# Loading the next batch's context, x and first two weights during the last MLP, and waiting for the stores one batch later

## What is computed

```
x = L0(x, ctx)   # x1 = LN(x) Wq, ctx Wk, ctx Wv, 16 heads; + x; then LN and an MLP of 2048, + residual
x = L1(x, ctx)   # 32 query heads on 8 key heads, additive mask, + x, then LN with gamma and beta
x = L2(x, ctx)   # LN(ctx) as keys and values; x + tanh(gate) * out
x = L3(ctx, x)   # keys and values over [ctx, x], queries from x; RMSNorm, MLP of 2048, + x
```

## Time and profile before

| | |
|---|---|
| median of 3 runs | 4301.14 us (4297.38 to 4302.05) |
| the profiled execution's own time | 4311.11 us |
| its span, first to last instruction | 4309.5 us |
| busy: PE, DVE, ACT, POOL | 87%, 35%, 27%, 7% of the span |
| mean granted TensorE clock | 0.943 of full |
| transfers of the 16 DMA engines | 271.10 MB, 63 GB/s mean |

### The profile page before, as it was taken

How to read it: one execution, slowest core, us unless ns; L and a number is a source line. 1 busy time by engine, 2 the same in 40 slices (tenths; PEclk the granted TensorE clock), 3 DMA queues, 4 the chain that set the end, 5 groups by cost and what they waited for, 6 DMA issues and landing times. The chain is left out here.

```text
span 4309.5 us, 39566 instructions
## 1 busy us (share of the span) xinstructions
PE 3736.4 (87%) x14128; PEld 1798.2 (42%) x14128; DVE 1525.2 (35%) x2792; ACT 1183.0 (27%) x1404; POOL 293.4 (7%) x228
## 2 busy tenths in 40 slices
PE   5998988889799898878979989887897989988799
PEld 2444533334344553333434455333343445533334
DVE  2415443530340544343034054434303305443430
ACT  1312323241131232324113133222412313322340
POOL 3000011000100001100010000110001000011000
PEclk9999999999899999989989999998998999999899
DMA  6322153311622215331162221533116221153401
GB/s 125 66 88 40 21 103 48 59 32 50 126 68 82 36 23 101 47 64 28 51 126 65 84 34 26 99 55 59 25 54 128 66 82 31 25 99 55 68 16 59
DMA packets 151761, 271.10 MB, mean 63 GB/s; under 512 B 15520, under 2 KB 22372, under 8 KB 151544
## 3 DMA queue, kind: packets, MB, share of 16 engines
q1 hardware_dynamic: 151556, 268.35, 30.8%
HBM read 152.95 MB, written 4.19 MB: 36 GB/s over the span
## 5 line engine op out<-in xcount | busy, mean ns | idle before, releaser
L908 ACT ACTIVATE pt<-score_banks 128x1024 f32<-128x1024 f32 x768 | 761.0, 1022 | 950.3 <-PE score_banks L769 482.4
L639 PE MATMUL bank<-xT,w 128*128 128x512 f32 x1664 | 755.4, 601 | 38.3 <-ACT xT L881 23.4
L1038 DVE TENSOR_REDUCE mcol<-bank 128x1 f32<-128x512 f32 x528 | 359.3, 689 | 469.7 <-PE bank L737 466.2
L639 PEld LDWEIGHTS bank<-xT,w 128*128 128x128 f32 x1664 | 315.9, 192 | 396.5 <-issue 370.4
L765 PE MATMUL score_banks<-qs,ks 99*128 99x512 f32 (+1 forms) x1280 | 450.7, 429 | 23.6 <-DMA qs<-nm_lo 12.6
L737 PE MATMUL bank<-ks,qs 97*128 97x512 f32 (+1 forms) x784 | 344.8, 453 | 137.7 <-DMA ks<-k_full 49.5
L1021 DVE TENSOR_REDUCE mcol<-score_banks 128x2 f32<-128x1024 f32 x248 | 301.7, 1223 | 426.2 <-PE score_banks L728 411.6
L838 PE MATMUL score_banks<-w,wide 128*128 128x512 f32 x1024 | 443.4, 592 | 0.0
L1035 DVE CUSTOM_DVE_ANT_0 bank<-bank,wide 128x512 f32<-128x512 f32 x416 | 284.7, 708 | 260.5 <-PE bank L737 259.9
L737 PEld LDWEIGHTS bank<-ks,qs 97*128 97x128 f32 (+1 forms) x784 | 155.0, 198 | 396.2 <-issue 349.1
L728 PE MATMUL score_banks<-ks,qs 97*128 97x512 f32 x496 | 275.4, 639 | 46.5 <-issue 23.8
(11 more groups left out here) (110 smaller groups left out, 3003.3 us busy)
## 6 DMA issues: line engine op xcount, KB each, us to landing
ks<-k_high SPq DMA_DIRECT2D x136, 256.0 KB, 5.7
w<-in_up SPq DMA_DIRECT2D x32, 1024.0 KB, 5.0
w<-in_down SPq DMA_DIRECT2D x32, 1024.0 KB, 5.3
qs<-q_high SPq DMA_DIRECT2D x112, 256.0 KB, 6.7
ks<-k_full SPq DMA_DIRECT2D x72, 256.0 KB, 7.8
w<-in_v SPq DMA_DIRECT2D x16, 1024.0 KB, 5.4
w<-in_q SPq DMA_DIRECT2D x16, 1024.0 KB, 8.1
qs<-q_full SPq DMA_DIRECT2D x64, 256.0 KB, 6.0
```

The costliest lines, as they stand in the source:

```text
L639: last = nc.tensor.matmul(o[:, :], wt[:, c, cols[0]:cols[1]], src[:, c, :], start=(c == 0), stop=(c == NC - 1))
L908: nc.scalar.activation(pt[:, i % PTB], score_banks[:, 2 * (i % 2):2 * (i % 2) + 2, :], ACT.Exp, scale=L.scale).then_inc(exp_done, 1)
L1038: ins = nc.vector.tensor_reduce(col, bank[:, :], AX.X, ALU.max)
```

## The change

Context and `x` of the next batch are loaded in steps down0 and down1 of the last MLP, and the first two weights of the next batch as soon as their slots are free (after up3 and after down2). `x` of a new batch now arrives in `xn`, which is `v[:, 4:8]`, and layer 0 reads it there. For batch 0 these four loads stand before the loop, ahead of the constants, and all engines pass them before the loop. The batch ends with a wait for those four loads (`next_in`). The stores are waited for by SP in the next batch, after it has issued the masks and the third weight; it then clears `out_stored` and raises `x_free`, which VectorE waits for before it writes `x` for the first time. After the loop a block of its own waits for the last stores. The host appends a copy of batch 0 to `x` and `ctx_2048`, so that the last batch too has a next one to load.

```diff
+        xn = v[:, NT:2 * NT, :]
...
             @block.sync
             def _(sp):
+                sp.dma_start(cx, A["ctx_2048"][0].rearrange("(t p) d -> p t d", p=P)).then_inc(first_in, 16)
+                sp.dma_start(xn, A["x"][0].rearrange("(t p) d -> p t d", p=P)).then_inc(first_in, 16)
+                for i in range(AHEAD):
+                    sp.dma_start(weight_slot(i), weight_source(i)).then_inc(first_in, 16)
                 for dst, src in CONSTS:
                     sp.dma_start(dst, src, allow_slow_non_contiguous=True).then_inc(const_in, 16)
+                sp.sem_inc(out_stored, 16 * NT)
+                sp.wait_ge(first_in, 16 * (2 + AHEAD))
...
-                    sp.dma_start(cx, tokens(A["ctx_2048"])).then_inc(ctx_in, 16)
-                    sp.dma_start(x[:, :, :], tokens(A["x"])).then_inc(x_in, 16)
                     sp.dma_start(m8[:, :], A["mask8"][bass.ds(b, 1), :]).then_inc(keymask_in, 16)
...
-                    for i in range(WSLOTS):
+                    for i in range(AHEAD, WSLOTS):
                         load_weights(i)
+                    sp.wait_ge(out_stored, 16 * NT)
+                    nc.sync.sem_clear(out_stored)
+                    sp.sem_inc(x_free, 1)
                     sp.wait_ge(keymask_set, 1)
...
+                        elif kind == "down" and n == 3 and step[2] < 2:
+                            sp.wait_ge(norm_done, N_NORM[("norm", 3, "mid")])
+                            if step[2] == 0:
+                                sp.dma_start(cx, tokens(A["ctx_2048"], b + 1)).then_inc(next_in, 16)
+                            else:
+                                sp.dma_start(xn, tokens(A["x"], b + 1)).then_inc(next_in, 16)
-                        if step in LAST_USE and LAST_USE[step] + WSLOTS < len(WEIGHTS):
-                            load_weights(LAST_USE[step] + WSLOTS)
+                        if step in LAST_USE:
+                            i = LAST_USE[step] + WSLOTS
+                            if i < len(WEIGHTS):
+                                load_weights(i)
+                            elif i - len(WEIGHTS) < AHEAD:
+                                wait_weights_used(sp, *WEIGHTS[i - WSLOTS])
+                                sp.dma_start(weight_slot(i - len(WEIGHTS)), weight_source(i - len(WEIGHTS))).then_inc(next_in, 16)
...
-                    sp.wait_ge(out_stored, 16 * NT)
+                    sp.wait_ge(next_in, 16 * (2 + AHEAD))
...
-                                ins = nc.vector.tensor_tensor(dst, bank[:, :], x[:, t, :], ALU.add)
+                                if (n, t) == (0, 0):
+                                    dve.wait_ge(x_free, 1)
+                                ins = nc.vector.tensor_tensor(dst, bank[:, :], (xn if n == 0 else x)[:, t, :], ALU.add)
...
+        with nc.Block() as block:
+            @block.sync
+            def _(sp):
+                sp.wait_ge(out_stored, 16 * NT)
```

More of the change, by code:

```diff
@@ L44 @@
 RING = 2
+AHEAD = 2
 class Layer:
@@ L283, in build @@
         gate_set = ctx.enter_context(nc.semaphore("gate_set"))
-        x_in, ctx_in, mask_in, out_stored = sem("x_in"), sem("ctx_in"), sem("mask_in"), sem("out_stored")
+        first_in = ctx.enter_context(nc.semaphore("first_in"))
+        out_stored = ctx.enter_context(nc.semaphore("out_stored"))
+        next_in, x_free = sem("next_in"), sem("x_free")
+        ctx_in, mask_in = sem("ctx_in"), sem("mask_in")
         keymask_in = sem("keymask_in")
@@ L451, in build, with weight_source, weight_slot @@
         CONSTS.append((gate[:, :], bcast(A["L2_xattn_gate"], 1)))
+        def weight_source(i):
+            n, name = WEIGHTS[i]
+            if name[:2] == "up":
+                f = int(name[2:])
+                src = A[f"up{n}"][:, f * D:(f + 1) * D]
+            elif name[:4] == "down":
+                f = int(name[4:])
+                src = A[f"down{n}"][f * D:(f + 1) * D, :]
+            else:
+                src = A[f"{name[0]}{n}"]
+            return src.rearrange("(c p) n -> p c n", p=P)
+        def weight_slot(i):
+            return w[:, i % WSLOTS, :, 0:weight_source(i).shape[2]]
         with nc.Block() as block:
@@ L619, in _ @@
                 def _(pe):
-                    landed = [0]
+                    landed = [AHEAD]
                     def need_weight(n, name):
@@ L625, in need_weight @@
                             k = landed[0]
-                            pe.wait_ge(w_in[k % WSLOTS], 16 * (k // WSLOTS + 1))
+                            pe.wait_ge(w_in[k % WSLOTS], 16 * (k // WSLOTS + (k % WSLOTS >= AHEAD)))
                             landed[0] += 1
@@ L653, in _ @@
                             if kind == "ctxT":
-                                pe.wait_ge(ctx_in, 16)
                                 src, c = cx, step[1]
@@ L956, in norm @@
                         if what == "ctx":
-                            dve.wait_ge(ctx_in, 32)
-                        if what == "x":
-                            dve.wait_ge(x_in, 16)
+                            dve.wait_ge(ctx_in, 16)
                         if what == "out":
                             dve.wait_ge(gamma_in, 32)
-                        src = cx if what == "ctx" else (v if (n, what) == (3, "mid") else x)
+                        src = cx if what == "ctx" else (v if (n, what) == (3, "mid") else xn if what == "x" else x)
                         dst = {"out": x, "ctx": cx}.get(what, zrow)
@@ L1157 @@
         a[k] = np.ascontiguousarray(a[k].reshape(-1, P).T)
+    for k in ("x", "ctx_2048"):
+        a[k] = np.concatenate([a[k], a[k][:1]])
     nc = bacc.Bacc("TRN2", target_bir_lowering=False, num_devices=1, dynamic_dma_scratch_size=1024)
```

17 lines of the change are left out of this document (4 added, 13 removed).

## The result

The changed kernel takes 4254.83 us (median of 4 runs, 4247.73 to 4257.18) against 4301.6 us before: a ratio of 0.9887, 95% interval 0.987 to 0.9904. Over all launches of this study the kernel before has a mean of 4298.7 us (66 launches) and the changed one of 4255.5 (8 launches), 43.2 us apart. The kernels were run in five sets, each beside launches of the kernel before, whose mean was 4302.1, 4300.5, 4295.6, 4297.2 and 4302.0 us in them: so two kernels are best compared within a set.

What follows compares the result with a forecast made beforehand. TensorE, busy 87% of the span, was taken as the bound, its longest wait being for the context at batch starts. Gains of 28.7 + 5.1 + 1.0 = 34.8 us take 4301.14 to 4266 us, range 4257 to 4279.

Steps and rivals of the forecast that it cites:

- 28.7 + 5.1 + 1.0 = 34.8 us: Gains: 28.7 from context and weights at batch starts, 5.1 from the stores' wait at three boundaries, 1.0 at launch end.
- the 1.7 that the prediction asked for: At each boundary the batch start should come 1.7 us sooner behind the last store, without SP's wait for its landing.
- fastest that the two chains allow: Batch start: with an early clock VectorE bounds, xT starts 13.3 us after ScalarE's first instruction; 4 us more gained in all.
- Rival 2: Batch start: masks land as late as before, 6.3 us, so VectorE's chain bounds xT; 4279 us; chance 0.10.
- Behind that point the work is the same before and after.: From the first xT transpose of each batch onward, the work was taken as the same before and after.
- rival 5: Inside batches: a shifted start moves the clock's dips and the kernel gets slower, above 4309 us; chance 0.02.
- Rival 1: Batch start: TensorE's code load is on the path, 4.4 us lost, 4270 us; chance 0.13.
- Rival 3: Before the loop: the four early loads delay the constants over 7.7 us and hold the loop; 4271 to 4276 us; chance 0.08.
- Rival 4: Batch start: TensorE stays at half clock through v and into q and k, no measurable gain, 4298 us; chance 0.03.

Runs made afterwards that it cites:

- c_weights_late: Changed kernel with only context and x loaded early, all three weights at the batch's start; 4276.79 us, ratio 0.9945.
- v_gap: Changed kernel, everything loaded early, but TensorE waits for VectorE before the first v matmul; 4274.36 us, ratio 0.9951.
- d_clears130: Changed kernel with 130 more semaphore clears at the end of each batch; 4287.56 us.
- a_wait_stores: Changed kernel, but SP again waits for the stores at the end of each batch; 4260.91 us, ratio 0.9916.
- d_clears46: Changed kernel with 46 more semaphore clears at the end of each batch; 4263.2 us.
- w_weights_only: Changed kernel with only the two weights loaded early, context and x again issued at the batch's start; 4286.83 us, ratio 0.998.
- f: Changed kernel with the list of semaphores cleared by one instruction instead of one each; 4245.09 us, ratio 0.9884.
- h: Changed kernel with one clear for all semaphores and the key mask rows worked out behind the two v tiles; 4239.97 us, ratio 0.9869.

## Why the prediction was wrong

The direction and the gain on the path were right; the sum was 8 to 12 us short, because the time behind the path was taken as fixed, and the range was too narrow by 2 us at its low end.

- **The path.** Forecast 28.7 + 5.1 + 1.0 = 34.8 us; the rest in the profiles fell by 35.4. By terms it is 29.7 + 4.4 + 1.4, so small errors cancel. TensorE idles 9.5, 9.3 and 9.5 us at the boundaries (forecast 9.3); `v` takes 9.2, 9.4 and 9.2 us up to `xT` behind them (9.4); `xT` starts at T0 + 13.3, 14.0, 14.2 and 14.8 in the four batches (14.3). T0 comes 1.3, 1.4 and 1.7 us sooner behind the last matmul, and 1.3 behind the last store at the first boundary: mostly under the 1.7 that the prediction asked for, though SP's wait for `out` is gone from the loop. Taking away the stores' wait alone gained 5.5 us by the medians, putting it back cost 6.8 on the path (6.1 forecast for it).
- **Batch 0** ran its `v` matmuls at full clock, 7.10 us, so there VectorE's chain is what `xT` waits for, 1.58 us. That is the forecast's "fastest that the two chains allow", T0 + 13.3, in one batch of four. Rival 2 is thereby half right about the mechanism and wrong about the landing: 3.1 us at the boundary (1085.84 - 1082.71), just at the point where it decides, against my 2.1, and over the 3 us that the prediction had named as a sign of being wrong. Behind a boundary TensorE, at half clock, was still the later of the two.
- **The step that failed** is "Behind that point the work is the same before and after." The work is, its time isn't. The bodies, which the sum put at no change, are about 2 us shorter each: 7.8 us in four batches by all launches (4146.3 - 4138.5), 13.1 and 4.5 in the two sets. Removing the wait for weight v, which I counted as 1.2 us and the clock of `v` alone, removes a pause of TensorE early in the batch, and c_weights_late and v_gap, which have such a pause again, have the long bodies again. That makes the pause the likeliest cause; it isn't shown to be the only one, since the change also takes 7 us of idle time from each boundary (d_clears130). I had priced the clock inside the bodies only as a risk (rival 5), with a spread of 3.3 us a batch, and gave it no gain.
- **The clock at the start.** It rises inside 1090 to 1092 in batch 1 (mean 0.55, so near 1091.8), and 4.6 us of `v` still ran at full clock, where it was 3.9 before the change. Windows of the changed kernel:

```profile
1078.00:1080.00 2.00, 0.00 (x0) 0.00 (x0) 0.00 (x0) 0.00 (x0) 0.00 (x0) 0.54 0.10 25
...
1090.00:1092.00 2.00, 2.00 (x4) 0.87 (x3) 1.52 (x5) 0.00 (x0) 0.26 (x1) 0.55 0.04 10
```

- **Rival 1**, the code load on the path, did not come: TensorE starts 0.25 us behind ScalarE in batch 1, and 0.3 and 1.0 in batches 2 and 3 (in batch 3 ScalarE is the early one; TensorE's idle time is 9.5 us as elsewhere). A q8 packet as in the earlier trace rows (that row doesn't say whose code it is) comes in batch 1 only at 1083.8 to 1084.0, a microsecond after TensorE's first matmul at 1082.71, and none lies between 1080 and it, so the first matmuls don't need it:

```profile
q8 instruction: 1, 0.02, 30.1%
```

  The rule of the Trainium skill, Runtime: NRT & Kernel Launch, Instruction fetch mechanics, is not refuted by it. A load that the branch has to wait for would lie before T0, where no run here separates it.
- **Rival 3**, late constants, was closer than thought: `gtanh` moved from 17.5 to 24.5, 7.0 us, not 5, with 7.7 of cover. It stayed hidden by 0.7 us.
- **Rival 4** did not come. Of **rival 5** the shifting half-clock stretches came, as a gain and not as a loss.

**What stays open.** Why the bodies are shorter. Behind the pauses before q the half-clock matmuls are seen at once. With a pause before `v` nothing of the kind is seen at the start of the body: that it costs half-clock stretches later is inferred from the means of two kernels against their neighbours, and followed in no trace; the changed kernel, without the pause, has the same stretches in some of its batches, as in the window of the result. Whether a long idle time at the boundary does the same as the pause is not separated, and no run puts one without the other into the kernel before.

## What to carry to other kernels

Add up the path by stages, and then ask of each wait that goes whether it was a pause of a busy TensorE: in this kernel a pause of 1 to 4 us in front of the q matmuls cost, beside itself, 1.7 to 3 us more in matmuls partly at half clock; a pause in front of `xT` showed no such cost. When launches of one kernel scatter by 20 us, split every profile into the stretch that the edit touches and the stretch that it doesn't, and compare those, before an explanation is sought for the total. Compare kernels that ran in one set: the kernel before moved by up to 6.5 us from set to set, nearly the size of the effect that was looked for. And when kernels are sorted by a feature, look for that feature in every profile: a_wait_stores and d_clears46 had the pause of w_weights_only and not its time. A load that is to go under other work must be early enough by what it takes to land alone (here 6.8 us for the weight, not 4 to 5.5): with context and `x` early the medians show 23.3 us gained, with the two weights early 9.6, where all four loads together give 40 to 47; each includes the 5.5 of the stores.

## What was not expected of the hardware

- The same program on the same inputs took from 4252.39 to 4272.0 us (a_wait_stores), and the kernel before from 4285.55 to 4310.69 over 66 launches; in the profiles single bodies of the same work differ from 1027 to 1042 us, with a mean granted clock of 0.960 in the shortest and 0.946 in the longest.
- A pause of 1.0 us in front of dense matmuls was followed by eight matmuls in 5.38 to 5.40 us in place of 3.67, in all four batches.
- Ten small transposes and 5.4 us of idle time did not keep the clock up across the boundary, while the 16 `v` matmuls ran at full clock (7.1 us) behind 10.8 to 11.8 us of idle time in a_wait_stores and d_clears46. Behind the 6.4 to 9.5 us at the boundaries of the changed kernel, f and h they took 8.8 to 9.4. In batch 0, where TensorE starts after 26 us without a matmul, they took 7.1, right behind the 16 transposes, in some launches (the changed kernel's first profile, h_one_clear_masks) and 9.0 in the changed kernel's second.
- Clearing the list of semaphores by one instruction instead of one for each took 2.5 to 3.0 us off each boundary: TensorE's idle time fell from 9.3 to 9.5 us to 6.5 to 6.8.
